# Row sums of an attention's exponentials taken from the ScalarE accumulator instead of a column of ones in the values

## The chip, the cores and the metric

The kernel runs on one core of one Trainium2 chip. The metric is the device time of one execution in microseconds (us). The kernel before has a median of 976.95 us over 3 runs (974.88 to 978.48).

## The reference

Eight batches of 512 tokens of width 256 go through gated cross attention and a gated mixture of experts:

```
x = x + tanh(g_xattn) * (softmax(q k^T / 8) v @ Wo + bo)     # q from layernorm(x), k and v from ctx; 16 heads of 64
x = x + tanh(g_ffn) * sum_e comb[e] * (layernorm(x) @ W_e^T + b_e)   # 8 experts, the best 2 by softmax
```

All inputs are float32. Per batch and head the scores are 512 x 512; the softmax divides each row of exponentials by its sum. Only this sum, and where its reciprocal is taken, are touched by the change.

## The kernel before

Every factor of the large matmuls is split into two float16 (or fp32r) parts, high and low, and each product is three matmuls (high-high, high-low, low-high).

A *unit* is a pair of heads by 128 queries. There are 32 units in a batch (8 pairs, 4 query tiles) and 256 in all. A unit goes through five engines:

- TensorE, `scores` (L1391): six matmuls into one of two PSUM buffers, `ST[u % 2]`, a bank for each head. It waits until the exponential of unit u-2 has released that buffer (`st_free`).
- VectorE, `maximum` (L941) and `shift_of` (L947): the negated row maximum, and the bias of the exponential.
- ScalarE, `exponential` (L762): two ACTIVATEs of 128x512, one for each head, from PSUM to `pf` in float32. The second one's end raises `st_free`. Later `probabilities` (L772) copies `pf` to float16 as the high part.
- GpSimd, `low` (L594): the low part. Then the SyncE queue transposes both parts by DMA into `pt_s`.
- TensorE, `values` (L1415), six units behind the scores: 24 matmuls (2 heads, 4 key tiles, 3 parts) of 65 columns each. Columns 0 to 63 are the head's values, column 64 is the column of ones (zero in the low part), so that the row sum falls out as the 65th output column in the PSUM bank `PV`.

Two units are a *half*. For each of the 128 halves VectorE runs `normalise`: it waits until TensorE has finished the values of both units (`pv_ready`), takes the reciprocal of the four sums from `PV` (L961), waits for its own result (`den_ready`) and multiplies (L964) into `o_n`, which releases `PV` (`o_ready`) and feeds the output projection.

The order of the work on each engine is static: five tables of 32 rows (`PE_ORDER`, `ACT_ORDER`, `DVE_ORDER`, `POOL_ORDER`, and the DMA loop) say what stands in each row beside that unit's own steps: projections for the next pairs, output projections, and the router and the experts of the batch before, as "jobs" that TensorE computes (L1242), ScalarE takes as a high part (`hi`: L677 to L692) and VectorE takes as a low part or adds (`take`). `NORMALISE_BACK = 3` puts `normalise` three halves behind its place. Batch 0 runs with its own extra work (splitting the weights, L754 and L1105), batches 1 to 6 run the full table, and the last one is followed by an epilogue.

At the start GpSimd writes constants; two of its memsets set the columns of ones and zeros in `v_s` (L551, L552). TensorE waits for the identity matrix, which is written behind them.

Of the kernel before, what the change touches and what calls it, by code (L numbers as in the profile page):

```python
# [33 lines left out]
P = 128  # L34
# [238 lines left out]
def build(nc, x, kv_t, g_xattn, g_ffn, wq, wk, wv, wo, bo, gate_t, expert_t, expert_b, out):  # L273
# [5 lines left out]
    with ctx:  # L279
        def sb(name, shape, dt=F32):  # L280
            return ctx.enter_context(nc.sbuf_tensor(name, shape, dt))
# [45 lines left out]
        kvin = sb("kvin", [P, TOKENS])  # L327
        kv_s = sb("kv_s", [P, 2, TOKENS], F32R)
        xt_s = sb("xt_s", [P, 2, LC, TOKENS], F16)
        v_s = sb("v_s", [P, 2, TT, HEADS, HEAD + 1], F16)  # L330
        QH = sb("QH", [P, SLOTS, TOKENS], F16)
        QL = sb("QL", [P, SLOTS, TOKENS], F16)
        KH = sb("KH", [P, SLOTS, TOKENS], F16)
# [20 lines left out]
        q_out = sb("q_out", [P, 2])  # L354
        half = sb("half", [P, 1])
        o_mul = sb("o_mul", [P, 2])
        rden = sb("rden", [P, TT])

        x2t_s = sb("x2t_s", [P, 2, LC, TOKENS], F16)
        acc = sb("acc", [P, TT, DIM])  # L360
# [86 lines left out]
                  ex_s[:, 1, c, 512 * k:512 * (k + 1)], 1) for c in range(LC) for k in range(EC)]  # L447
        assert len(late) == LATE

        CONST_POOL = EXPERTS + 11  # L450
        CONST_DVE = 2

        def run(row, before=None, after=None):
# [87 lines left out]
        def _(pool):  # L541
# [3 lines left out]
            for e in range(EXPERTS):  # L545
# [2 lines left out]
            pool.memset(zero[:, :], 0.0).then_inc(const_pool, 1)  # L548
            pool.memset(half[:, :], 0.5).then_inc(const_pool, 1)
            pool.memset(nmax[:, :, :, 1], P_SHIFT).then_inc(const_pool, 1)  # L550
            pool.memset(v_s[:, 0, :, :, HEAD:HEAD + 1], 1.0).then_inc(const_pool, 1)  # L551
            pool.memset(v_s[:, 1, :, :, HEAD:HEAD + 1], 0.0).then_inc(const_pool, 1)  # L552
            pool.wait_ge(const_pool, EXPERTS + 9)
            pool.affine_select(out=ident[:, :], in_=ident[:, :], compare_op=ALU.not_equal, fill=1.0, base=0,
                               pattern=[[-1, P]], channel_multiplier=1).then_inc(const_pool, 1)
            pool.wait_ge(const_pool, EXPERTS + 10)
            pool.tensor_tensor(fold[:, :], ident[0:2 * EXPERTS, 0:EXPERTS], ident[0:2 * EXPERTS, EXPERTS:2 * EXPERTS],
                               ALU.add).then_inc(const_pool, 1)

# [106 lines left out]
        def _(act):  # L666
            act.wait_ge(kv_in, 16)
            act.activation(kv_s[:, 0, :], kvin[:, :], ACT.Copy).then_inc(kv_hi, 1)
            def take_hi(it, name):

                act.wait_ge(job_ready, it.done(JOBS, name))
                m = SHARED[it.bank(name)]
                kind = name[0]
                of = it.batch(name)
                if kind == "q":
                    act.wait_ge(scale_ready, 2 * of + 2)
                    last = act.activation(QH[:, it.pair_slot(name), :], m[:, :], ACT.Copy,  # L677
                                          scale=q_out[:, of % 2:of % 2 + 1])
                elif kind == "k":
                    act.wait_ge(scale_ready, 2 * of + 2)  # L680
                    last = act.activation(KH[:, it.pair_slot(name), :], m[:, :], ACT.Copy,  # L681
                                          scale=k_mul[:, of % 2:of % 2 + 1])
                elif kind == "xt":
                    last = act.activation(xt_s[:, 0, name[1], :], m[:, :], ACT.Copy)
                elif kind == "x2t":
                    last = act.activation(x2t_s[:, 0, name[1], :], m[:, :], ACT.Copy)
                elif kind == "ot":
                    last = act.activation(ot_s[:, 0, name[1] % GROUP, :], m[:, :], ACT.Copy)
                else:
                    t, g = name[1:3]  # L690
                    act.wait_ge(scale_done, it.b + 1)
                    last = act.activation(v_s[:, 0, t, g * HH:(g + 1) * HH, 0:HEAD],  # L692
                                          m[:, :].rearrange("p (h d) -> p h d", d=HEAD), ACT.Copy,
                                          scale=v_mul[:, of % 2, 0:1])
                last.then_inc(job_hi, 1)
# [60 lines left out]
            def exponential(b, p, u):  # L756

                n = unit_count(b, p, u)
                act.wait_ge(shift_ready, n)
                act.wait_ge(p_lo, n)  # L760
                for i in range(2):
                    last = act.activation(pf[:, (n - 1) % PF_SLOTS, i, :], ST[u % 2][:, i, :], ACT.Exp,  # L762
                                          bias=shifts[:, u % 2, i:i + 1])
                last.then_inc(st_free, 1)

            def probabilities(it, p, u):
# [27 lines left out]
        def _(dve):  # L794
# [1 line left out]
            dve.memset(ones[:, :], 1.0).then_inc(job_free, BANKS)  # L796
            dve.memset(r1[:, :], 0.0).then_inc(st_free, 2)
            dve.memset(r2[:, :], 0.0).then_inc(p_lo, PF_SLOTS)
            dve.memset(rden[:, :], 0.0).then_inc(pv_ready, PT_SLOTS)
            dve.memset(rstd[:, :], 0.0).then_inc(o_ready, 1)  # L800
            dve.memset(p2[:, :, :], 0.0).then_inc(y_out, 16)

# [35 lines left out]
            def take(it, name):  # L838
# [78 lines left out]
                if kind in ("q", "k"):  # L917
                    h_s, l_s = (QH, QL) if kind == "q" else (KH, KL)
                    slot_, of = it.pair_slot(name), it.batch(name)
                    scale = (q_out if kind == "q" else k_mul)[:, of % 2:of % 2 + 1]  # L920
                    last = dve.scalar_tensor_tensor(l_s[:, slot_, :], m[:, :], scale, h_s[:, slot_, :],  # L921
                                                    ALU.mult, ALU.subtract)
                elif kind == "xt":
                    last = dve.tensor_tensor(xt_s[:, 1, name[1], :], m[:, :], xt_s[:, 0, name[1], :], ALU.subtract)
                elif kind == "x2t":
                    last = dve.tensor_tensor(x2t_s[:, 1, name[1], :], m[:, :], x2t_s[:, 0, name[1], :], ALU.subtract)
                elif kind == "ot":
                    s = name[1] % GROUP
                    last = dve.tensor_tensor(ot_s[:, 1, s, :], m[:, :], ot_s[:, 0, s, :], ALU.subtract)
                else:  # L930
                    t, g = name[1:3]
                    last = dve.scalar_tensor_tensor(v_s[:, 1, t, g * HH:(g + 1) * HH, 0:HEAD],  # L932
                                                    m[:, :].rearrange("p (h d) -> p h d", d=HEAD),
                                                    v_mul[:, it.b % 2, 0:1],
                                                    v_s[:, 0, t, g * HH:(g + 1) * HH, 0:HEAD],
                                                    ALU.mult, ALU.subtract)
                last.then_inc(job_free, 1)

# [10 lines left out]
            def normalise(it, p, half):  # L949

                b = it.b
                n = head_count(b, 2 * p + half)
                if half == 0 and p < 0:
                    dve.wait_ge(job_ready, it.start(JOBS))
                elif half == 0 and (p >= 2 or it.kind != FIRST):
                    dve.wait_ge(job_ready, it.done(JOBS, ("ot", (p - 2) % PAIRS)))
                outs = values_bank(it, p * TT + 2 * half)[:, 0:4 * (HEAD + 1)].rearrange("p (n d) -> p n d", n=4)
                dve.wait_ge(pv_ready, unit_count(b, p, 2 * half + 1) + PT_SLOTS)
                if it.kind == LAST and p == PAIRS - 1:
                    dve.wait_ge(o_ready, n)  # L960
                dve.reciprocal(rden[:, :], outs[:, :, HEAD]).then_inc(den_ready, 1)  # L961
                dve.wait_ge(den_ready, n)
                dst = o_n[:, p % 2, 2 * half:2 * half + 2, :].rearrange("p t (h d) -> p (t h) d", d=HEAD)
                dve.tensor_tensor(dst, outs[:, :, 0:HEAD], rden[:, :].unsqueeze(2).broadcast_to([P, TT, HEAD]),  # L964
                                  ALU.mult).then_inc(o_ready, 1)


            dve.wait_ge(x_half, 16)
# [266 lines left out]
        def _(pe):  # L1235
# [159 lines left out]
            def values(it, m):  # L1395

                b, p, t = it.b, m // TT, m % TT
                if it.kind == FIRST and m == 0:
                    pe.wait_ge(late_step, 1)
                if it.kind == LAST and m >= ON_PE:  # L1400
                    pe.wait_ge(tail_lo, m - ON_PE + 1)
                else:
                    pe.wait_ge(hi_turned[t], 16 * pair_count(b, p))
                    pe.wait_ge(lo_turned[t], 16 * pair_count(b, p))
                if it.kind == LAST and m == ON_PE:
                    pe.wait_ge(o_ready, head_count(b, HEADS - 2))
                elif t % 2 == 0 and (it.kind != LAST or m != ON_PE - 2):
                    pe.wait_ge(o_ready, head_count(b, 2 * p + t // 2))
                slot = it.ring(p, t, PT_SLOTS)
                for i in range(2):  # L1410
                    col = (t % 2 * 2 + i) * (HEAD + 1)
                    dst = values_bank(it, m)[:, col:col + HEAD + 1]
                    for k in range(TT):
                        for n, (a, c) in enumerate(((0, 0), (0, 1), (1, 0))):
                            last = pe.matmul(dst, pt_s[:, slot, a, i, k, :],  # L1415
                                             v_s[:, c, k, (2 * p + i) % HEADS, :],
                                             start=(k == 0 and n == 0), stop=(k == TT - 1 and n == 2))
                last.then_inc(pv_ready, 1)
# [109 lines left out]
```

## Time and profile before

| | us |
|---|---|
| median of 3 runs | 976.95 |
| the profiled execution's own time | 976.57 |
| its span, first to last instruction | 974.4 |
| TensorE (PE) busy | 924.9 (95%) |
| VectorE (DVE) busy | 855.0 (88%) |
| ScalarE (ACT) busy | 747.8 (77%) |
| GpSimd (POOL) busy | 639.9 (66%) |

In the profile PE is TensorE's matmuls and PEld its weight loads. "A <- B" behind an idle time says that engine A stood still until B's instruction had ended. The chain is the work that ended last, followed back from the end of the execution; "issue" in it is time in which nothing in the profile was waited for. One batch of the steady part takes 111.2 to 111.3 us.

### The profile page before, as it was taken

The numbers are of one execution on the slowest core, as the hardware profiler recorded it, in microseconds if no ns is written. First come the engines' busy times: TensorE is split into PE (matmuls) and PEld (weight loads), VectorE is DVE, ScalarE is ACT, GpSimd is POOL, SyncE is SP. The second block draws the span as 40 slices with busy tenths as digits, with TensorE's granted clock in tenths as the row PEclk, the third lists the DMA queues.
The fourth block names the chain that finished last, engine by engine and source line by source line (L and its number), as shares of the span: only waits on it lengthen the run. The fifth ranks groups of instructions, "written<-read, shape, count | busy, mean of one in ns | idle before, by whom it ended". The sixth has DMA issues, their size and how long they took to land.

```text
span 974.4 us, 28714 instructions
## 1 busy us (share of the span) xinstructions
PE 924.9 (95%) x11332; PEld 643.3 (66%) x11332; DVE 855.0 (88%) x1818; ACT 747.8 (77%) x1092; POOL 639.9 (66%) x439
## 2 busy tenths in 40 slices
PE   6678689999999999999999999999999999999997
PEld 4245456677667776677666776677766776677773
DVE  6877878998898988989899998999889998989868
ACT  3686889958898689958799588967899688967710
POOL 4364777958586876957677676858678585866600
PEclk8798899999999999999999999999999999999999
DMA  7486899989899899998999798999999899989910
GB/s 265 87 138 124 138 164 168 185 131 165 149 189 175 140 159 174 167 163 155 147 190 185 136 164 172 178 154 155 153 191 180 136 163 164 178 127 159 163 39 22
DMA packets 549141, 150.97 MB, mean 155 GB/s; under 512 B 537592, under 2 KB 547216, under 8 KB 548752
## 3 DMA queue, kind: packets, MB, share of 16 engines
q1 hardware_dynamic: 549008, 149.13, 90.6%
q8 instruction: 91, 1.49, 0.6%
q14 instruction: 42, 0.34, 0.1%
HBM read 11.70 MB, written 4.19 MB: 16 GB/s over the span
## 4 chain that ended last, share of the span: by engine, by line
PE 85%; DVE 7%; issue 3%; ACT 3%; POOL 1%; DMA 0%; SPq 0%; DVEq 0%; ACTq 0%; POOLq 0%
PE MB L1242 40%; PE PV L1415 19%; PE ST L1391 18%; PE MB L1254 5%; DVE nmax L941 2%; DVE acc L882 2%; ACT pf L762 1%; POOL p_s L594 1%; PE MB L1332 1%; PE MB L1327 1%; DMA kvin<-kv_t 0%; DVE wo_s L1105 0%; PE ST L1427 0%; PE MB L1339 0%; DVE QL L921 0%
## 5 line engine op out<-in xcount | busy, mean ns | idle before, releaser
L594 POOL TENSOR_TENSOR p_s<-pf,p_s 128x1024 f16<-128x1024 f32 x254 | 541.5, 2133 | 270.5 <-ACT p_s L772 222.7
L762 ACT ACTIVATE pf<-ST,shifts 128x512 f32<-128x512 f32 x512 | 322.9, 686 | 108.2 <-DVE shifts L947 107.8
L941 DVE TENSOR_REDUCE nmax<-ST 128x2 f32<-128x1024 f32 x256 | 310.3, 1217 | 21.9 <-PE ST L1391 20.1
L772 ACT ACTIVATE p_s<-pf 128x1024 f16<-128x1024 f32 x254 | 268.3, 1060 | 3.6
L1415 PEld LDWEIGHTS PV<-v_s,pt_s 128*128 128x128 f16 x6096 | 204.7, 98 | 45.4 <-issue 36.4
L1415 PE MATMUL PV<-v_s,pt_s 128*128 128x65 f16 x6096 | 218.9, 195 | 6.4 <-DVE o_n L964 5.0
L1242 PE MATMUL MB<-ex_s,x2t_s 128*128 128x256 f16 (+1 forms) x1380 | 165.5, 276 | 0.0
L1242 PEld LDWEIGHTS MB<-ex_s,x2t_s 128*128 128x128 f16 x1380 | 131.9, 98 | 20.4
L1391 PE MATMUL ST<-KH,QH 64*128 64x512 f16 x512 | 100.6, 390 | 16.5 <-ACT pf L762 14.8
L901 DVE SCALAR_TENSOR_TENSOR acc<-MB,m,acc 128x256 f32<-128x256 f32 x224 | 95.5, 475 | 3.9 <-PE MB L1242 3.0
L1391 PE MATMUL ST<-KH,QL 64*128 64x512 f16 x512 | 98.8, 382 | 0.0
L1391 PE MATMUL ST<-KL,QH 64*128 64x512 f16 x512 | 98.6, 382 | 0.0
L1242 PE MATMUL MB<-xt_s,wq_s 128*128 128x512 f16 x384 | 95.1, 385 | 0.0
L1242 PE MATMUL MB<-wo_s,ot_s 128*128 128x256 f16 x744 | 92.8, 276 | 0.0
L1242 PEld LDWEIGHTS MB<-wo_s,ot_s 128*128 128x128 f16 x744 | 70.9, 99 | 16.2 <-issue 4.6
L1391 PEld LDWEIGHTS ST<-KH,QH 64*128 64x128 f16 x512 | 24.8, 93 | 73.9 <-ACT pf L762 30.0
L1242 PE MATMUL MB<-kv_s,wk_s 128*128 128x512 f32 x192 | 62.8, 436 | 3.3 <-DVE v_s L932 2.3
L1242 PE MATMUL MB<-wv_s,kv_s 128*128 128x512 f32 x192 | 61.5, 438 | 4.0 <-DVE QL L921 4.0
L1242 PEld LDWEIGHTS MB<-xt_s,wq_s 128*128 128x128 f16 x384 | 33.7, 99 | 40.7 <-issue 10.8
L921 DVE SCALAR_TENSOR_TENSOR QL<-MB,q_out,QH 128x512 f16<-128x512 f32 x64 | 47.6, 743 | 13.7 <-ACT QH L677 13.6
L681 ACT ACTIVATE KH<-MB,k_mul 128x512 f16<-128x512 f32 x64 | 44.1, 689 | 18.5 <-PE MB L1242 18.3
L964 DVE TENSOR_TENSOR o_n<-PV,rden 128x256 f32<-128x256 f32 x127 | 53.9, 424 | 4.4
(160 smaller groups left out, 1021.5 us busy)
## 6 DMA issues: line engine op xcount, KB each, us to landing
pt_s<-p_s SPq DMA_TRANSPOSE x508, 3.4
xin<-x SPq DMA_DIRECT2D x7, 512.0 KB, 4.4
out<-acc SPq DMA_DIRECT2D x7, 512.0 KB, 3.7
kvin<-kv_t SPq DMA_DIRECT2D x8, 256.0 KB, 4.6
stage_e<-expert_t SPq DMA_DIRECT2D x1, 2048.0 KB, 13.5
stage_o<-wo SPq DMA_DIRECT2D x1, 1024.0 KB, 9.1
stage_q<-wq SPq DMA_DIRECT2D x1, 768.0 KB, 6.9
xin<-x SPq DMA_DIRECT2D x2, 256.0 KB, 2.9
```

The costliest lines, as they stand in the source:

```text
L594: pool.tensor_tensor(p_s[:, slot, 1, :, :], pf[:, it.ring(p, u, PF_SLOTS), :, :], p_s[:, slot, 0, :, :], ALU.subtract).then_inc(p_lo, 1)
L681: last = act.activation(KH[:, it.pair_slot(name), :], m[:, :], ACT.Copy, scale=k_mul[:, of % 2:of % 2 + 1])
L762: last = act.activation(pf[:, (n - 1) % PF_SLOTS, i, :], ST[u % 2][:, i, :], ACT.Exp, bias=shifts[:, u % 2, i:i + 1])
L772: act.activation(p_s[:, it.ring(p, u, P_SLOTS), 0, :, :], pf[:, it.ring(p, u, PF_SLOTS), :, :], ACT.Copy).then_inc(p_hi, 1)
L901: last = dve.scalar_tensor_tensor(acc[:, t, :], m[:, DIM * i:DIM * (i + 1)], comb[:, t, e:e + 1], acc[:, t, :], ALU.mult, ALU.add)
L921: last = dve.scalar_tensor_tensor(l_s[:, slot_, :], m[:, :], scale, h_s[:, slot_, :], ALU.mult, ALU.subtract)
L941: dve.tensor_reduce(nmax[:, t % 2, :, 0], ST[t % 2][:, :, :], AX.X, ALU.max, negate=True)\
L964: dve.tensor_tensor(dst, outs[:, :, 0:HEAD], rden[:, :].unsqueeze(2).broadcast_to([P, TT, HEAD]), ALU.mult).then_inc(o_ready, 1)
L1242: last = pe.matmul(dst, s, m, start=(k == 0), stop=(k == n - 1))
L1254: last = pe.transpose(bank_[:, tile(t)], src(t), ident[:, :])
L1391: last = pe.matmul(ST[t % 2][:, i, :], queries[r, s, tile(t)], keys[r, s, :], start=(n == 0), stop=(n == len(terms) - 1))
L1415: last = pe.matmul(dst, pt_s[:, slot, a, i, k, :], v_s[:, c, k, (2 * p + i) % HEADS, :], start=(k == 0 and n == 0), stop=(k == TT - 1 and ...
```

## The change

The values have 64 columns for each head, and there is no column of ones. The two exponentials of a unit each write the sum of their 512 outputs for each query into a new tile `den` (128 x 32 units x 2), through the accumulator output of ACTIVATE. The reciprocal is taken from `den` in a function `inverse`, which waits for the exponentials of its half and is called behind the multiply of the half before; `rden` has two buffers. Two memsets of GpSimd go.

```diff
-        v_s = sb("v_s", [P, 2, TT, HEADS, HEAD + 1], F16)
+        v_s = sb("v_s", [P, 2, TT, HEADS, HEAD], F16)
...
-        rden = sb("rden", [P, TT])
+        den = sb("den", [P, UNITS, 2])
+        rden = sb("rden", [P, 2, TT])
...
-            pool.memset(v_s[:, 0, :, :, HEAD:HEAD + 1], 1.0).then_inc(const_pool, 1)
-            pool.memset(v_s[:, 1, :, :, HEAD:HEAD + 1], 0.0).then_inc(const_pool, 1)
...
                     last = act.activation(pf[:, (n - 1) % PF_SLOTS, i, :], ST[u % 2][:, i, :], ACT.Exp,
-                                          bias=shifts[:, u % 2, i:i + 1])
+                                          bias=shifts[:, u % 2, i:i + 1],
+                                          accum_out=den[:, p * TT + u, i:i + 1])
                 last.then_inc(st_free, 1)
...
-                outs = values_bank(it, p * TT + 2 * half)[:, 0:4 * (HEAD + 1)].rearrange("p (n d) -> p n d", n=4)
+                outs = values_bank(it, p * TT + 2 * half)[:, 0:4 * HEAD].rearrange("p (n d) -> p n d", n=4)
                 dve.wait_ge(pv_ready, unit_count(b, p, 2 * half + 1) + PT_SLOTS)
...
-                dve.reciprocal(rden[:, :], outs[:, :, HEAD]).then_inc(den_ready, 1)
+                if n == 1:
+                    inverse(b, n)
                 dve.wait_ge(den_ready, n)
...
-                dve.tensor_tensor(dst, outs[:, :, 0:HEAD], rden[:, :].unsqueeze(2).broadcast_to([P, TT, HEAD]),
+                dve.tensor_tensor(dst, outs[:, :, :], rden[:, n % 2, :].unsqueeze(2).broadcast_to([P, TT, HEAD]),
                                   ALU.mult).then_inc(o_ready, 1)
+                if n < BATCHES * HEADS:
+                    inverse(b, n + 1)
+
+            def inverse(b, n):
+
+                first = (2 * n - 2) % UNITS
+                dve.wait_ge(st_free, 2 * n + 2)
+                dve.reciprocal(rden[:, n % 2, :], den[:, first:first + 2, :].rearrange("p t h -> p (t h)"))\
+                   .then_inc(den_ready, 1)
...
-                    col = (t % 2 * 2 + i) * (HEAD + 1)
-                    dst = values_bank(it, m)[:, col:col + HEAD + 1]
+                    col = (t % 2 * 2 + i) * HEAD
+                    dst = values_bank(it, m)[:, col:col + HEAD]
```

## Rows read from the trace of the kernel before

**Rows 1.** Chain by line, 577 to 688.3 us (one steady batch).

```profile
by line: PE MB L1242 49.3%; PE PV L1415 21.7%; PE ST L1391 20.7%; PE MB L1254 5.6%; PE MB L1332 0.9%; PE MB L1327 0.9%; PE MB L1339 0.6%; PE MB L1336 0.4%; PE MB L1319 0.1%
```

**Rows 2.** Stretches: window: length, PE, PEld, DVE, ACT, POOL busy, clock, DMA share, GB/s.

```profile
20.00:60.00 40.00, 26.62 (x206) 12.95 (x205) 30.05 (x52) 27.59 (x41) 17.16 (x9) 0.87 0.63 114
60.00:132.00 72.00, 54.95 (x634) 34.89 (x633) 59.32 (x103) 56.89 (x84) 44.59 (x30) 0.86 0.77 132
577.00:688.30 111.30, 111.30 (x1421) 78.76 (x1418) 101.53 (x220) 91.65 (x135) 80.08 (x54) 1.00 0.97 165
910.80:974.40 63.60, 55.60 (x562) 38.62 (x559) 47.78 (x112) 15.69 (x23) 10.13 (x8) 0.98 0.34 62
```

**Rows 3.** The same view inside that batch.

```profile
598.50:630.40 31.90, 31.90 (x432) 20.97 (x430) 29.51 (x58) 31.66 (x47) 25.68 (x19) 1.00 1.06 191
641.30:664.00 22.70, 22.70 (x285) 17.47 (x285) 21.11 (x61) 12.40 (x19) 12.07 (x10) 1.00 0.90 134
664.00:688.30 24.30, 24.30 (x315) 17.83 (x313) 22.42 (x44) 21.00 (x32) 19.93 (x17) 1.00 0.94 160
```

**Rows 4.** The same view of the exponentials (L762) alone: ScalarE busy, clock, DMA, GB/s.

```profile
598.50:630.40 31.90, 13.97 (x22) 1.00 1.06 191
```

**Rows 5.** Waits, 577 to 688.3 us: total us, times, longest us.

```profile
PEld ST L1391 <- ACT pf L762: 1.6, 4, 0.4
```

**Rows 6.** Pieces of the chain, 688.3 to 800 us: start, length, what.

```profile
688.80 2.62 PE MB L1242 x24
...
715.52 1.29 PE MB L1242 x6
716.82 1.47 PE PV L1415 x48
```

**Rows 7.** Groups: busy us, mean ns | idle before.

```profile
L762 ACT ACTIVATE pf<-ST,shifts 128x512 f32<-128x512 f32 x512 | 322.9, 686 | 108.2 <-DVE shifts L947 107.8
L1415 PE MATMUL PV<-v_s,pt_s 128*128 128x65 f16 x6096 | 218.9, 195 | 6.4 <-DVE o_n L964 5.0 <-issue 0.9 <-DVE v_s L932 0.5
```

**Rows 8.** Timeline: the shortest ACTIVATE, and a pair of exponentials.

```profile
22.46 0.19 ACT L712 ACTIVATE tg<-gates 128x2 f32<-128x2 f32 x1
24.32 1.27 ACT L762 ACTIVATE pf<-ST,shifts 128x512 f32<-128x512 f32 x2 [1.67 <-DVE shifts L947]
```

**Rows 9.** Timeline at 629 us: an exponential, and the scores that need its buffer.

```profile
629.07 1.26 ACT L762 ACTIVATE pf<-ST,shifts 128x512 f32<-128x512 f32 x2
...
630.74 0.39 PE L1391 MATMUL ST<-KH,QH 64*128 64x512 f16 x2
```

**Rows 10.** Timeline of VectorE at 506 and 508 us.

```profile
506.57 0.16 DVE L947 TENSOR_REDUCE shifts<-nmax 128x2 f32<-128x4 f32 x1
506.65 1.41 DVE L806 BATCH_NORM_STATS2 stats<-acc 128x6 f32<-128x256 f32 x4
...
508.39 0.15 DVE L961 RECIPROCAL rden<-PV 128x4 f32<-128x4 f32 x1
...
508.57 0.42 DVE L964 TENSOR_TENSOR o_n<-PV,rden 128x256 f32<-128x256 f32 x1
```

**Rows 11.** Timeline of the start.

```profile
1.87 0.57 POOL L552 MEMSET v_s<- 128x64 f16 x1
...
3.04 5.21 PE L1427 MATMUL ST<-ident 128*128 128x128 f32 x30 [3.04 <-POOL ident L554]
...
6.88 2.33 DVE L821 TENSOR_SCALAR xn<-xin,mv,rstd 128x256 f32<-128x256 f32 x4
...
7.97 0.25 PEld L1254 LDWEIGHTS MB<-ident,xn 128*128 128x128 f32 x2
```

**Rows 12.** Chain from 20 to 132 us: first and last of nine exponential pieces over 0.5 us.

```profile
27.96 0.68 ACT pf L762
...
129.08 1.16 ACT pf L762 x2
```

More of the change, by code:

```diff
@@ L448, in build @@
         assert len(late) == LATE
-        CONST_POOL = EXPERTS + 11
+        CONST_POOL = EXPERTS + 9
         CONST_DVE = 2
@@ L550, in _ @@
             pool.memset(nmax[:, :, :, 1], P_SHIFT).then_inc(const_pool, 1)
-            pool.memset(v_s[:, 0, :, :, HEAD:HEAD + 1], 1.0).then_inc(const_pool, 1)
-            pool.memset(v_s[:, 1, :, :, HEAD:HEAD + 1], 0.0).then_inc(const_pool, 1)
-            pool.wait_ge(const_pool, EXPERTS + 9)
+            pool.wait_ge(const_pool, EXPERTS + 7)
             pool.affine_select(out=ident[:, :], in_=ident[:, :], compare_op=ALU.not_equal, fill=1.0, base=0,
                                pattern=[[-1, P]], channel_multiplier=1).then_inc(const_pool, 1)
-            pool.wait_ge(const_pool, EXPERTS + 10)
+            pool.wait_ge(const_pool, EXPERTS + 8)
             pool.tensor_tensor(fold[:, :], ident[0:2 * EXPERTS, 0:EXPERTS], ident[0:2 * EXPERTS, EXPERTS:2 * EXPERTS],
@@ L691, in take_hi @@
                     act.wait_ge(scale_done, it.b + 1)
-                    last = act.activation(v_s[:, 0, t, g * HH:(g + 1) * HH, 0:HEAD],
+                    last = act.activation(v_s[:, 0, t, g * HH:(g + 1) * HH, :],
                                           m[:, :].rearrange("p (h d) -> p h d", d=HEAD), ACT.Copy,
@@ L798, in _ @@
             dve.memset(r2[:, :], 0.0).then_inc(p_lo, PF_SLOTS)
-            dve.memset(rden[:, :], 0.0).then_inc(pv_ready, PT_SLOTS)
+            dve.memset(rden[:, 0, :], 0.0).then_inc(pv_ready, PT_SLOTS)
             dve.memset(rstd[:, :], 0.0).then_inc(o_ready, 1)
@@ L931, in take @@
                     t, g = name[1:3]
-                    last = dve.scalar_tensor_tensor(v_s[:, 1, t, g * HH:(g + 1) * HH, 0:HEAD],
+                    last = dve.scalar_tensor_tensor(v_s[:, 1, t, g * HH:(g + 1) * HH, :],
                                                     m[:, :].rearrange("p (h d) -> p h d", d=HEAD),
                                                     v_mul[:, it.b % 2, 0:1],
-                                                    v_s[:, 0, t, g * HH:(g + 1) * HH, 0:HEAD],
+                                                    v_s[:, 0, t, g * HH:(g + 1) * HH, :],
                                                     ALU.mult, ALU.subtract)
```

## The prediction

> **What bounds the kernel now.** I first read the chain of one steady batch [rows 1]: every percent of it is TensorE, so in batches 1 to 6, and nearly in batch 7, the time is TensorE's work and no wait. In the same 111.3 us VectorE is busy for 101.5, ScalarE for 91.7 and GpSimd for 80.1 [rows 2]. That looks like 20 us of room on ScalarE, and the change puts its new work there, so I cut the batch into stretches [rows 3]. The room isn't spread evenly. From 598.5 to 630.4 us ScalarE is busy for 31.66 of 31.90 us: for a third of the batch it is as full as TensorE. The room lies behind: 10.3 us from 641.3 to 664.0, then 3.3 us to the end. The second thing to see is how closely the two engines are coupled. The exponential at 629.07 ends at 630.33, and the scores that overwrite its PSUM buffer start at 630.74 [rows 9]: 0.41 us of slack at the end of the full stretch. The waits agree [rows 5]: four times in a batch the scores already wait for an exponential, 1.6 us in all, though TensorE's pipeline covers it. Before 132 us the chain leaves TensorE and passes through exponentials, nine pieces over 0.5 us with 13 ACTIVATEs in them and five shorter ones [rows 12]. At the end ScalarE is busy for 15.7 of the last 63.6 us [rows 2].
>
> The sum is made against the profiled execution, 976.57 us (span 974.4 and 2.2 around it). It is 0.4 below the median of 976.95.
>
> **Narrower matmuls (a gain).** 256 units x 24 = 6144 value matmuls lose one column of 65 (6096 of them are in one group [rows 7], 48 in another bank). Forty-eight take 1.47 us [rows 6], 30.6 ns each, of which 65 columns at 2.4 GHz (granted clock 1.00 [rows 2]) are 27.1. A column is 0.417 ns; 6144 are 2.6 us, on TensorE's chain and so in full, 0.32 us in a batch. Larger only if the rest shrinks too: 256 columns take 109.2 ns and 512 take 215 [rows 6], 2.5 and 1.7 ns over their columns, where 65 have 3.5. If 64 columns took 26.7 + 2.5 = 29.2 ns, the gain would be 1.4 ns x 6144 = 8.6 us. I take 2.6, bounds 0 and 8.6.
>
> The Trainium skill (TensorE: Matmul & The Clock Gate, "Back-to-back issue gap") gives about 60 cycles, 25 ns, for 1 to 64 columns; by that a value matmul would lose 5.6 ns and the sum 34 us. No row here has such a float16 matmul, and the page's own formula for wider ones, N/2.4 + 2.5, gives 29.2 at 64. I count it as a rival with a small chance.
>
> **The accumulator output (a loss).** The trace has no ACTIVATE that writes a sum, so its price must be bounded, for 512 exponentials. Below: nothing, if the sum is written in the shadow of the next ACTIVATE. Nearest row: a sum of 128x1 is written by something like the shortest ACTIVATE, 0.19 us [rows 8]. Two exponentials in a row take 1.27 us, not 2 x 0.686 [rows 7, 8], so an ACTIVATE hides 0.10 us behind its neighbour, and a short one of 0.19 would add 0.09. Above: if the read has to wait until the exponential has drained, the overlap is lost too, 0.19 + 0.10 = 0.29 us. I take 0.09, since nothing speaks for the loss of an overlap that all neighbours here have, and keep 0 and 0.29.
>
> The skill says of VectorE (VectorE: DVE Perf Modes, "Two Vector instructions with no wait between them") that an instruction with an accumulator output is two, the main one and a read of the accumulator. If ScalarE does the same, the lower bound of nothing falls away; no row here can show it.
>
> **What it does to a batch.** The full stretch holds 11 units, that is 22 exponentials (14.0 of its 31.7 us [rows 4]). They add 22 x 0.09 = 2.0 us to ScalarE, it has 0.24 us idle that it can't count on, and the scores at its end can give 0.41: they come 1.57 us late, and the batch with them, for nothing later gives TensorE time back: its chain has no wait to shrink. After that ScalarE has room again. Of the four waits I take two outside the stretch, each growing by the two reads in front of it: 2 x 0.18 = 0.36. The columns bring 0.32 a batch, but only where TensorE bounds, two thirds: 0.21. Net +1.72 us a batch, and the batches 1 to 7 give +12.0. In batch 0, 18 exponentials of the chain add 0.09 each, 1.6, and the narrower matmuls take off some 0.3: +1.3. The end, with ScalarE so little busy, I leave at 0.
>
> **Reciprocals ahead (nearly nothing).** Now VectorE starts the reciprocal at 508.39, waits for it, multiplies at 508.57 [rows 10]: 0.18 us on the path from the last value matmul to `o_ready`. Afterwards the multiply starts at once, and the reciprocal costs what a small instruction costs with no wait behind it, 0.08 from start to start (506.57 to 506.65 [rows 10]). 0.10 us less for each of 128 halves is 12.8 us of VectorE, but VectorE doesn't bound: in the full stretch it is busy for 29.5 of 31.9, in front of ScalarE's queue of ready work. Value matmuls wait for `o_n` 5.0 us in the whole run [rows 7], and each such wait can shrink by 0.18 at the most. I take 0, bounds -1.5 and 0. The added wait (`st_free`) stands in front of all that VectorE does later, the maxima and shifts first, and ScalarE would wait for those. But the order puts the exponentials of that half at least two rows, 7 us, before it; it should never hold.
>
> **Start.** Without the memsets (0.57 us, L552) the identity is written earlier, and TensorE's warm-up starts before 3.04. The transposes behind it start at 7.97 and in the end wait for VectorE's fourth tile at 9.21 [rows 11], which doesn't move: 0, bounds -0.5 and 0. `v_s` is written in instructions of the same sizes: 0.
>
> **Sum.** 976.57 + 12.0 + 1.3 = 989.9: 990 us, 1.3% slower.
>
> **The rivals.**
> - *The read is hidden (974 us).* Only the columns are left: -2.6. For it: 19.4 us of idle ScalarE in a batch outside the stretch, and with a price under 0.02 us the 0.41 us of slack covers all 22. Against it: a result that is written has to be issued.
> - *Faster, by the matmuls (968 us).* The excess of 3.5 ns over the columns is due to 65 odd columns at odd addresses, goes to 2.5, and the read is nearly free: -8.6. It wins only where the price is under 0.02 us as well, since in the full stretch ScalarE would otherwise set the time. The page's 25 ns belongs here: on rows, 34 us off TensorE can't be had, as VectorE's 101.5 us in a batch leave 9.8, and ScalarE's full stretch none; the time would be some 960.
> - *The read drains ScalarE (1010 us or more).* At 0.19 us the stretch grows by 22 x 0.19 - 0.41 = 3.8, the other waits by 0.76, less 0.2: 4.3 x 7 = 30.4, and batch 0 by 3.1: 1010. At 0.29 it is 7.0 x 7 + 5 = +54, 1030. ScalarE's batch would then be 91.7 + 64 x 0.29 = 110.3, the batch itself. For it: the sum is only known when the last element is through.
> - *The change isn't what it says:* `inverse` waits after all and holds VectorE. The two rows of distance speak against it; each hold would delay a maximum by its length, and with one of 0.5 us a batch the time is 980 where the read is free.
>
> **Chances.** The forecast 0.45 (its own range 981 to 1003, prices of 0.04 to 0.15 us), hidden read 0.25, faster matmuls 0.14 (0.02 of it for the page's rule), draining read 0.13, a holding wait 0.03. The range reaches over both sides, 969 to 1012. A measurement of this kernel tells about 0.5% (5 us) from no change. Faster by more: 0.17, the faster matmuls and a hidden read with some luck at batch 0. Within: 0.27, the hidden read and the lower edge of the forecast. Slower: 0.56.
>
> **What would show it.** The stretch from 598 to 630 of a batch: ScalarE full, longer by 1.6 us, and the scores waiting for exponentials for 2 us or more a batch; the chain with ScalarE pieces there. A second instruction behind each exponential, or 1.27 us for a pair grown to 1.45. Value matmuls, 48 of them in 1.45 us (29.2 each would be 1.40). Between reciprocal and multiply no wait, and none in front of the reciprocal. I am wrong if a pair of exponentials still takes 1.27 us, or if the pair grows and yet the chain of a batch stays TensorE alone: then the order has more give than the 0.41 us that I read.

## The result and the profile after

The changed kernel takes 986.75 us (986.15 to 987.01, 4 runs) against 977.42 for the kernel before: a ratio of 1.0098, 95% interval 1.0078 to 1.0119. It is slower by 1.0%; the forecast was 990 us, 1.3% slower, and the measured time lies in its range. The profiled execution is the one of 986.15 us, with a span of 984.3. All times and ratios here are of executions at a granted clock of 0.98; one of the kernel with seven units moved (below) ran at 0.555, took 1511.6 us and is left out.

The page of the changed kernel, engines with busy us and share of the span; then its groups (busy us, mean ns, idle before), where a new kind of instruction appears:

```profile
PE 923.8 (94%) x11332; PEld 636.1 (65%) x11332; DVE 848.8 (86%) x1818; ACT 788.0 (80%) x1604; POOL 639.5 (65%) x437
...
L761 ACT ACTIVATE pf<-ST,shifts 128x512 f32<-128x512 f32 x512 | 347.5, 691 | 91.9 <-DVE shifts L947 89.7
...
L1425 PE MATMUL PV<-v_s,pt_s 128*128 128x64 f16 x6096 | 210.8, 194 | 5.0 <-DVE o_n L965 4.4
...
L761 ACT ACTIVATION_READ_ACCUMULATOR pf<-ST,shifts 128x1 f32 x512 | 107.5, 210 | 0.0
```

ScalarE has 512 instructions more, 1604 for 1092, and is busy for 40 us more (788.0 for 747.8). Its timeline shows what one of them costs:

```profile
605.47 0.68 ACT L761 ACTIVATE pf<-ST,shifts 128x512 f32<-128x512 f32 x1
606.04 0.20 ACT L761 ACTIVATION_READ_ACCUMULATOR pf<-ST,shifts 128x1 f32 x1
606.13 0.69 ACT L761 ACTIVATE pf<-ST,shifts 128x512 f32<-128x512 f32 x1
606.70 0.21 ACT L761 ACTIVATION_READ_ACCUMULATOR pf<-ST,shifts 128x1 f32 x1
```

The read lasts 0.20 to 0.21 us but overlaps both neighbours. It starts 0.57 us after the exponential, while that one still runs, and the next exponential starts 0.09 us after the read: 0.66 us from one to the next, where the kernel before has 0.57. So the read starts where the next exponential used to, and pushes it back by the 0.09 us that it occupies. A pair with its reads takes 1.44 us (605.47 to 606.91) where it took 1.27 [rows 8].

The chain of a batch, which was TensorE to the last percent [rows 1], now leaves it (by line, 582 to 694.4 us; then one piece of two batches, from which a batch is (548.56 - 323.80) / 2 = 112.4 us):

```profile
by line: PE MB L1252 24.8%; ACT pf L761 15.9%; issue 13.4%; PE PV L1425 11.6%; PE ST L1401 8.6%; ACT p_s L772 7.1%; POOL p_s L593 3.8%; DVE nmax L941 3.2%; PE MB L1264 3.1%; ACT QH L676 1.2%; ACT v_s L691 1.1%; DVE KL L921 1.1%; PE MB L1342
...
323.80 6.55 PE MB L1252 x60
548.56 6.55 PE MB L1252 x60
```

The stretch that was full [rows 3] is 32.9 us long for 31.9, and ScalarE is busy for 32.84 of it (columns as in [rows 2]). The exponential at its end, which ended 0.41 us ahead of the scores [rows 9], is followed by its read at 637.64 and ends at 637.92, 0.15 us ahead:

```profile
604.80:637.70 32.90, 31.94 (x433) 20.56 (x431) 29.16 (x58) 32.84 (x69) 25.82 (x19) 1.00 1.10 189
```

```profile
637.64 0.28 ACT L761 ACTIVATION_READ_ACCUMULATOR pf<-ST,shifts 128x1 f32 x1
...
638.07 0.39 PE L1401 MATMUL ST<-KH,QH 64*128 64x512 f16 x2
```

The scores wait for exponentials twelve times in a batch, where they did four times [rows 5] (waits, 582 to 694.4 us: total, times, longest):

```profile
PEld ST L1401 <- ACT pf L761: 5.5, 12, 0.8
```

And the value matmuls are quicker by more than a column: 48 mostly take 1.40 to 1.42 us in the chain, where they mostly took 1.44 to 1.47 [rows 6].

```profile
586.34 1.40 PE PV L1425 x48
635.70 1.42 PE PV L1425 x48
```

### The profile page after: what moved, and what is told of

Its sections match the earlier page's. It is cut to its first block, busy times and chain, and to the rows that moved or that the text cites. A ratio compares the mean times of both kernels' runs of the same rounds, so it can differ in the third digit from the quotient of the medians.

```text
span 984.3 us, 29283 instructions
## 1 busy us (share of the span) xinstructions
PE 923.8 (94%) x11332; PEld 636.1 (65%) x11332; DVE 848.8 (86%) x1818; ACT 788.0 (80%) x1604; POOL 639.5 (65%) x437
## 4 chain that ended last, share of the span: by engine, by line
PE 50%; ACT 20%; issue 14%; DVE 9%; POOL 7%; DMA 0%; ACTq 0%; SPq 0%; DVEq 0%; POOLq 0%
PE MB L1252 23%; ACT pf L761 12%; PE PV L1425 10%; PE ST L1401 9%; POOL p_s L593 6%; ACT p_s L772 4%; PE MB L1264 3%; DVE nmax L941 3%; DVE acc L882 2%; ACT QH L676 1%; ACT v_s L691 1%; DVE KL L921 1%; PE MB L1342 1%; PE MB L1337 1%; DVE QL L921 1%
## 5 line engine op out<-in xcount | busy, mean ns | idle before, releaser
L761 ACT ACTIVATE pf<-ST,shifts 128x512 f32<-128x512 f32 x512 | 347.5, 691 | 91.9 <-DVE shifts L947 89.7
L1425 PEld LDWEIGHTS PV<-v_s,pt_s 128*128 128x128 f16 x6096 | 197.2, 99 | 43.9 <-issue 32.0
L1425 PE MATMUL PV<-v_s,pt_s 128*128 128x64 f16 x6096 | 210.8, 194 | 5.0 <-DVE o_n L965 4.4
L761 ACT ACTIVATION_READ_ACCUMULATOR pf<-ST,shifts 128x1 f32 x512 | 107.5, 210 | 0.0
L932 DVE SCALAR_TENSOR_TENSOR v_s<-MB,v_mul,v_s 128x512 f16<-128x512 f32 x64 | 46.8, 744 | 16.5 <-ACT v_s L691 16.2
```

The lines of the kernel that those rows point to most:

```text
L1425: last = pe.matmul(dst, pt_s[:, slot, a, i, k, :], v_s[:, c, k, (2 * p + i) % HEADS, :], start=(k == 0 and n == 0), stop=(k == TT - 1 and ...
```

## The experiments

Medians are in us; in brackets stands the ratio to the kernel before with its 95% interval. The runs were made in groups, each with the kernel before in it; in the first group that has 976.59.

**No sums.** The changed kernel without the accumulator output; `den` is a constant, so the output isn't normalised.

```diff
-                                          accum_out=den[:, p * TT + u, i:i + 1])
+            pool.memset(den[:, :, :], 16384.0).then_inc(const_pool, 1)
```

> The changed kernel without the accumulator output: the exponentials write no sums, and the reciprocals are taken of a constant, so the output isn't normalised. It leaves the 64 columns and the reciprocals ahead. Theory A (the reads cost what they cost, the columns give one column each): 2.6 us less than before, about 974.5. Rival (the narrower matmuls also lose their excess over the columns): 8.6 us less, about 968.5. If it comes out above 977, something other than the reads makes the changed kernel slow.

Measured: 969.77 (0.9931, 0.9917 to 0.9944), 6.8 us less than before. That lies near the rival's 968.5 and not near the 974.5 of theory A: I gave the columns 2.6 us. The chain of its batch is TensorE alone again, and its value matmuls have the new length:

```profile
by line: PE MB L1252 49.9%; PE PV L1425 21.3%; PE ST L1401 20.5%; PE MB L1264 5.5%; PE MB L1342 0.9%; PE MB L1337 0.9%; PE MB L1349 0.6%; PE MB L1346 0.4%; PE MB L1329 0.1%
...
599.13 1.40 PE PV L1425 x48
601.83 1.40 PE PV L1425 x48
```

I counted their steps from start to start, between value matmuls that follow each other directly, from 140 to 900 us. Before: a mean of 30.43 ns, three quarters of them at 28 to 31 and 1191 of 5118 at 32 to 36. Here and in the changed kernel: 29.30, and none at 32 to 36. 1.13 ns x 6144 = 6.9 us is the whole gain.

**Reads alone.** The kernel before, with `accum_out=den[:, p * TT + u, i:i + 1]` added to the exponentials. Nothing uses `den`.

> The kernel before with the accumulator output added to the exponentials and nothing else; nobody uses the sums. Theory A (512 reads of 0.09 us on ScalarE, felt in the stretch where ScalarE is full): before plus what the change lost and what the columns gave back, 9.6 + 2.6 = 12 us, about 989.5. Rival (the reads are cheap, and the loss comes from the new place of the reciprocals or the new layout of the values): within 3 us of before.

Measured: 993.95 (1.0177, 1.0164 to 1.0190), 17.4 us more, 0.034 us for each read. The rival is out. The loss is larger than the 12 that I expected, for I had reckoned it as the change's loss plus the gain of the columns, and that gain is 6.8 and not 2.6. The line of the score waits reads as in the changed kernel:

```profile
PEld ST L1393 <- ACT pf L763: 5.5, 13, 0.8
```

**Reads in rows 0 to 11, and in rows 12 to 31.** As before, but `accum_out=(... if p * TT + u < 12 else None)`, and `>= 12`.

> As the kernel before with the accumulator output, but only for the units in rows 0 to 11 of each batch, 24 of 64 reads, where ScalarE has no idle time. Theory A (the loss is made where ScalarE is full): two thirds or more of the loss of the kernel with all reads, 8 us or more over before. Rival B (each read delays the release of a score buffer by the same time, wherever it stands): 24/64 of the loss, 4.5 us.

> As the kernel before with the accumulator output, but only for the units in rows 12 to 31 of each batch, 40 of 64 reads. Theory A: a third of the loss or less, 4 us over before, for the more reads stand where ScalarE has idle time. Rival B: 40/64 of the loss, 7.5 us.

Measured: early 985.01 (1.0082, 1.0068 to 1.0096), late 985.57 (1.0089, 1.0076 to 1.0102). The losses, 8.4 and 9.0 us, add up to the 17.4 of all reads. Both theories miss, and the rival by less: the early reads make 48% of the loss, where they are 37.5% of the reads and theory A wanted two thirds. 24 early reads in a batch cost 0.044 us each, 40 late ones 0.028: a read in the full stretch costs half as much again, but late reads are far from free. The waits of the scores (582 to 694 us) grow in both: nine weight loads of the scores wait instead of four. First the early reads, then the late ones:

```profile
PEld ST L1393 <- ACT pf L763: 3.9, 9, 0.7
PE ST L1393 <- ACT pf L763: 0.5, 2, 0.3
```

```profile
PEld ST L1393 <- ACT pf L763: 3.5, 9, 0.8
PE ST L1393 <- ACT pf L763: 0.3, 1, 0.3
```

The trace of the kernel before shows a reason. The exponential of a late row, unit 21, ends at 673.15, and the scores that need its buffer start at 673.20: 0.05 us, far less than the 0.41 at the end of the full stretch [rows 9]. Unit 29 has 0.05 too, units 19 and 27 have 0.33, and the least in the full stretch is 0.30.

```profile
671.90 1.25 ACT L762 ACTIVATE pf<-ST,shifts 128x512 f32<-128x512 f32 x2
...
673.20 0.39 PE L1391 MATMUL ST<-KH,QH 64*128 64x512 f16 x2
```

Between the starts of a batch's first scores and the next batch's I read 111.25 us before, 112.38 with early reads, 112.07 with late ones and 113.23 with all. So per batch it is 1.13 and 0.82. Of the rest of the late ones' loss, 3.8 us lie in batch 0 (130.9 us from its first scores to the next batch's, for 127.1 before) and 2.4 behind the last batch's first scores.

**Where does the column's extra gain come from?** In this group "before" has 976.20, in the next 976.73, and beside the four chosen units at the end 976.82. First 64 columns without sums as above, but the values laid out at 65 elements for each head:

```diff
-        v_s = sb("v_s", [P, 2, TT, HEADS, HEAD], F16)
+        v_s = sb("v_s", [P, 2, TT, HEADS, HEAD + 1], F16)
```

> The kernel without sums (64 columns, reciprocals ahead of a constant, so the output isn't normalised), but with the values laid out at 65 elements for each head as before, so that every second head starts 2 bytes off a 4-byte boundary. In the kernel before a quarter of the value matmuls take 32 to 36 ns from start to start instead of 28 to 31; with 64 columns none do. If the start address is the cause, they come back: a mean of 30.0 or more, and the time rises from 969.8 to 974 or more. If the odd count of columns is the cause, the mean stays at 29.3 and the time within 2 us of 969.8.

Measured: 971.88 (0.9952, 0.9938 to 0.9966), and the mean step is 29.88 ns, between the two that I had named: 877 of 5098 steps are at 32 to 36. Then the kernel before, column of ones and all, at 66 and at 96 elements for each head:

```diff
-        v_s = sb("v_s", [P, 2, TT, HEADS, HEAD + 1], F16)
+        v_s = sb("v_s", [P, 2, TT, HEADS, 66], F16)
```

> The kernel before with one column of padding behind each head's 65 values, so that every head starts on a 4-byte boundary; all else, the column of ones too, as before. If the start address makes the slow steps: the mean step falls from 30.4 to 29.7 ns, and the time by 0.7 x 6144 = 4.4 us, to about 972. If the count of 65 does: no change, 976.6.

> The same with 96 elements for each head: every head starts on a 64-byte boundary. If a 4-byte boundary is enough, the same as with 66. If the slow steps come from heads that lie across a larger boundary (16 or 64 bytes), it is this kernel that loses them, 972, and the one with 66 keeps some. If the count of columns does it: 976.6.

Measured: 976.23 (0.9999, 0.9989 to 1.0009) and 976.63 (1.0002, 0.9991 to 1.0013): nothing. In the second one the slow steps aren't spread over 32 to 36 any more, they are all at 34 to 36, 1092 of 5121, and the mean is 30.58. Values in the chain, first 66 and then 96:

```profile
602.77 1.45 PE PV L1415 x48
```

```profile
603.18 1.46 PE PV L1415 x48
```

So the start address is no cause of its own: with 65 columns every tried start has the slow steps. With 64 they are gone where the heads follow each other at 128 bytes, and where they do at 130 half of the excess is back. The slow steps aren't scattered, either. At 96 elements, 94% of them come exactly five steps behind the one before, at 66 elements 77% do, and in the kernel before 85% come four or five behind. The steps between are 29.2 ns in all three, which is what 64 columns take. So 65 columns mostly run at the speed of 64 and lose some 5 ns at every fourth or fifth matmul. What makes that step is still open.

**The reciprocal in its old place.** The changed kernel with `inverse(b, n)` in front of the multiply of its own half, and the same in the kernel without sums.

```diff
-                if n == 1:
-                    inverse(b, n)
+                inverse(b, n)
...
-                if n < BATCHES * HEADS:
-                    inverse(b, n + 1)
```

> The changed kernel with the reciprocal taken where it was, right in front of the multiply of its own half, still of the sums of the accumulator. The document's step gives the place of the reciprocals nothing: within 1.5 us of the changed kernel, 986 to 988.5. Rival (the reciprocals ahead take 0.1 us off VectorE 128 times, and ScalarE waits for VectorE's shifts for 90 us): 4 us or more slower than the changed kernel, 991.

> The kernel without sums (64 columns, output not normalised) with the reciprocal in front of the multiply of its own half. It closes a square with the kernel without sums (969.8), the changed kernel (986.75) and the one that has its reciprocals not ahead (990.2). If the reciprocals ahead help only where ScalarE sets the time, because they bring VectorE's shifts forward: within 1.5 us of 969.8. If they shorten TensorE's own path: 3.5 us more, 973.3. The steps of the matmuls (29.3 ns for 30.4) alone give 6.9 us less than before, 969.5.

Measured: 990.23 with sums (1.0141, 1.0126 to 1.0156) and 970.22 without (0.9936, 0.9923 to 0.9949). Taking the reciprocals ahead is worth 3.5 us in the changed kernel (4.2 if each is taken against the kernel before of its own group) and 0.5, which these runs can't tell from nothing, where ScalarE has no reads. The first lies near its rival's 991, the second is what I expected if they help only where ScalarE sets the time, and had the 3.5 us been TensorE's own path, the kernel without sums would have lost them too. What the timeline shows saved is time of VectorE. Here is the timeline of the kernel with its reciprocals not ahead, then of the changed one:

```profile
503.09 0.18 DVE L971 RECIPROCAL rden<-den 128x4 f32<-128x4 f32 x1
503.31 0.42 DVE L964 TENSOR_TENSOR o_n<-PV,rden 128x256 f32<-128x256 f32 x1
503.65 0.74 DVE L921 SCALAR_TENSOR_TENSOR QL<-MB,q_out,QH 128x512 f16<-128x512 f32 x1
```

```profile
500.81 0.42 DVE L965 TENSOR_TENSOR o_n<-PV,rden 128x256 f32<-128x256 f32 x1 [0.23 <-PE PV L1425]
501.15 0.17 DVE L974 RECIPROCAL rden<-den 128x4 f32<-128x4 f32 x1
501.23 0.72 DVE L921 SCALAR_TENSOR_TENSOR QL<-MB,q_out,QH 128x512 f16<-128x512 f32 x1
```

From the first of the two to what follows it is 0.56 us in the one and 0.42 in the other; the medians of all 128 halves are 0.55 and 0.43. In the whole run ScalarE waits 92.4 us for shifts in the one and 89.7 in the other, and the value matmuls 5.1 and 4.4 for `o_n`. Which of the two makes the 3.5 us was not tried.

**Giving ScalarE its time back.** The changed kernel, complete; for some units of each batch GpSimd makes the float16 copy that ScalarE made.

```diff
+                if p * TT + u in MOVED:
+                    pool.wait_ge(st_free, unit_count(it.b, p, u) + 2)
+                    pool.tensor_copy(p_s[:, slot, 0, :, :], pf[:, it.ring(p, u, PF_SLOTS), :, :]).then_inc(p_moved, 1)
```

> The changed kernel, complete, but for the units of rows 0, 2 and 4 of each batch GpSimd makes the float16 copy of the exponentials that ScalarE made (1.07 us each). GpSimd stands idle there for 6 us in the changed kernel. Theory (the reads cost time because ScalarE is full in rows 0 to 11): ScalarE gets 3.2 us back there, more than the 2.2 of its 24 reads, and the time falls by what 24 early reads had cost, some 8 us, to 979. Rival (GpSimd's copy is as slow as its subtraction, 2.1 us, and the low parts, the transposes and the release of pf become late): no gain or a loss, 987 or more.

> The same for the units of rows 0, 2, 4, 18, 21, 27 and 30. Theory: the later reads are paid back too, 972 or less, faster than before. Rival: as above, and more of it.

> As the kernel in which GpSimd copies the units of rows 0, 2 and 4, but with rows 3, 6, 10 and 20: the copies that stand right in front of exponentials whose end the scores wait for (units 4, 7, 11 and 21 of a batch, slack 0.06 to 0.23 us in the changed kernel, with ScalarE behind its shifts by 0.5 to 3.2 us). Theory (only a copy in front of a late exponential pays): faster than with rows 0, 2 and 4, 979 or less. Rival (the later low parts and transposes of the moved units cost as much): 981 to 984.

Measured: three units 981.60 (1.0054, 1.0041 to 1.0067), seven units 983.0 (1.0067, 1.0054 to 1.0080), the four chosen ones 980.08 (1.0025, 1.0015 to 1.0034). I had expected 979, 972 and 979. Relieving ScalarE takes back 5 to 7 of the 17 us that the reads cost with three and four units, which supports the theory that its time is what they cost; with seven it is 4, no better than with three. The copy isn't slow on GpSimd. With the four units the chain of a batch goes through its subtraction (L605) for a third, so GpSimd may have become late in its turn. That isn't shown, since the kernel with its reciprocals not ahead has 25% of it there and moves nothing. The group of the copies, then the chain:

```profile
L601 POOL CAST p_s<-pf 128x1024 f16<-128x1024 f32 x32 | 33.7, 1053 | 1.5 <-ACT pf L773 1.5
```

```profile
by line: POOL p_s L605 32.9%; issue 18.8%; PE MB L1266 17.4%; PE ST L1415 6.9%; PE PV L1439 6.6%; ACT pf L773 2.6%; PE MB L1278 2.4%; POOL p_s L601 1.8%; POOL xn L581 1.4%; DVE o_mul L1004 1.1%; DVE nmax L955 1.0%; ACT p_s L786 1.0%; POOL r
```

By the profiled executions the four units make a steady batch 111.4 us long, for 112.38 in the changed kernel and 111.25 in the kernel before. Batch 0 stays at 131.7, for 130.7 and 127.1: what is left of the loss against the kernel before stands there.

No version of these beats the kernel before.

## Why the prediction was right, and where it was not

Four kernels, each one step from the next, split the change: 64 columns -6.5 us (976.7 to 970.2), reads +20.0 (to 990.2), reciprocals ahead -3.5 (to 986.75). The parts depend on each other: the reads cost 17.4 with 65 columns and 17.0 with 64 and the reciprocals ahead (969.8 to 986.75). The kernel before has medians of 976.2 to 977.4 in the groups, so each part is known to about 1 us. Point by point:

- **Price of a read: right.** I took 0.09 us from the shortest ACTIVATE less the overlap; measured are 0.09 from its start to the next exponential's, with a duration of 0.21. Neither bound, 0 and 0.29, was near. The Trainium skill's rule that an instruction with an accumulator output is two (VectorE: DVE Perf Modes, "Two Vector instructions with no wait between them") is stated there of VectorE. It holds for ScalarE here: the trace names the second one.
- **What the reads do to a batch: the sum right by luck, the place half wrong.** I had 1.57 + 0.36 = 1.93 us a batch; reads alone cost 113.23 - 111.25 = 1.98. But the early rows alone cost 1.13 and the late ones 0.82, so two errors cancel. The step that failed is "After that ScalarE has room again", with two waits taken for the late rows. Busy time over 24 us hid that single exponentials there have as little slack as in the full stretch or less, 0.05 us at units 21 and 29. The early term was too large: I let all 22 reads pile up, and the stretch grew by 1.0, not 1.57.
- **Net of a batch:** forecast were +1.72 us, measured are +1.13 (111.25 to 112.38). The columns give 0.81 (I had 0.21), the reads cost 2.25 on top of them (1.93), and the reciprocals give 0.31 (0).
- **Batch 0: mis-sized.** I gave the reads 1.6 us there. In the traces of the kernel before and of the reads alone it takes 127.1 and 131.7 us, 4.5 more, while batches 1 to 6 together make 10.6 (two of them take 112.2 and 112.4 us in the kernel before) and the last one 2.0. The early reads alone add 1.1 to batch 0 and the late ones alone 3.8. Its chain runs through ScalarE and VectorE by turns; what delays it beyond the 18 reads that I counted isn't shown.
- **Columns: a term mis-sized by 4.7 us.** I took 0.417 ns for each matmul, 2.6 us, and let only 1.8 of them into the sum (0.21 a batch and 0.3); measured are 1.13 ns and 6.5 to 6.9 us. Their excess over the columns (30.6 against 27.1 ns) stood in my rows, with the right bound behind it (29.2 ns; measured 29.3), and I took the small value. The Trainium skill's N/2.4 + 2.5 ns for isolated matmuls (TensorE: Matmul & The Clock Gate, "Back-to-back issue gap") agrees with the 29.3; its 25 ns for up to 64 columns doesn't.
- **Reciprocals ahead: mis-sized.** I took 0 with bounds -1.5 and 0; they give -3.5. The 0.10 us that I worked out for each half is 0.13 to 0.14 by the timeline. The step "VectorE doesn't bound" held before the change, and holds without sums (0.5 us). With the reads, ScalarE and VectorE stand in the chain of a batch. I take it that the loop of scores, maximum, shift, exponential and scores then bounds both, but no run tests it by itself. The new wait did not hold: the one idle time in front of a reciprocal, 1.6 us, is that of the first half, which waits for its values.
- **Start: 0 as taken.** The warm-up starts at 2.44 for 3.04, and the first transposes stand at 8.70 for 7.97; the batch's first scores start within half a microsecond of before.
- **The sum.** It had +15.1 for the reads (1.93 x 7 + 1.6), -1.8 for the columns and 0 for the reciprocals. The four kernels give +20.0, -6.5 and -3.5. Gains that were 4.7 and 3.5 too small and a loss that was 4.9 too small leave 3.3 us: 990 for 986.75. The forecast's side rests on the read's price; the nearness of the number rests on errors that cancel. One rival was summed wrong: a holding wait of 0.5 us a batch with a free read comes to about 977.5 or 978 by my own terms and not to 980, for I had left the 2.6 us of the columns out.

What the prediction named as its test came true: a pair of exponentials grown to 1.44 us (I had named 1.45) with a second instruction behind each, a fuller stretch at ScalarE, and a chain with ScalarE in it. The 2 us or more of score waits are 5.5. The 48 value matmuls, for which I had named 1.45 us, take 1.40 to 1.42.

## What to carry to other kernels

An accumulator output on ScalarE isn't free: it is an instruction more, 0.09 us of the engine here, and on an engine that feeds a tight loop 512 of them cost 17 us, two and a half times what dropping a column from 6144 matmuls gave back. Before you give an engine new work, read the slack of each step that others wait for (end of the exponential to start of the scores), all of them and not at the fullest place alone; busy shares by stretch overlook it. Where a small matmul takes more than its columns by more than its wider neighbours do, measure that excess by itself: a change of one column can remove it.

## What the runs showed of the hardware that I had not expected

- `ACTIVATION_READ_ACCUMULATOR` lasts 0.21 us and occupies ScalarE for 0.09.
- Float16 value matmuls of 65 columns take a slow step of 32 to 36 ns in one of four or five, with heads at 130, 132 or 192 bytes, mostly at every fourth or fifth matmul; with 64 columns at 128 bytes there are none, and with 64 columns at 130 bytes one in six. What makes them stays open: neither the count of columns nor the start address alone does.
- GpSimd copies 128x1024 from float32 to float16 in 1.05 us, as quickly as ScalarE (1.07), but takes 2.13 for the subtraction of the same size.
